# Graph sums by slots: four transfers per part and a new division of the 98 edge chunks

## The chip, the cores and the metric

The kernel runs on one core of a Trainium2 chip. The metric is the device time of one execution in microseconds (us). The engines are named as in the profile: PE (matmul) with PEld (its weight loads), DVE (VectorE), ACT (ScalarE), POOL (GpSimd) and SP (SyncE, which here only issues DMA transfers). The core has 16 DMA engines, which all queues share.

## The reference

A graph layer with 6250 nodes of 64 features and 200,000 edges of 64 features. The edges are sorted by `dst`; `src` is in no order.

```python
in_agg = segment_sum(edge_feat, receivers, num_segments=6250)   # receivers = dst
out_agg = segment_sum(edge_feat, senders, num_segments=6250)    # senders = src
to_updater = concatenate([in_agg, out_agg, node_feat], axis=1)  # 192 wide
h = relu(to_updater @ W1 + b1)                                  # 256 wide
x = layernorm(x + h @ W2 + b2)
```

Nearly all of the time goes into the two segment sums. The sum by `dst` is cheap, because a chunk of sorted edges touches a narrow window of nodes. The sum by `src` is the hard one: its rows have to reach nodes all over the table.

## The kernel before

The edges are cut into 98 chunks of 2048, laid out as 128 partitions by 16 columns. Every chunk is split into three bf16 parts that add up to the fp32 value (`split_hi`, `split_rest`, `split_mid`, `split_lo`), and its sum by `dst` is one set of 48 matmuls against a one-hot of the window (`sum_windows`, line 1632). For the sum by `src` there are two ways.

- *Scattered.* Within one column, edges with the same node are added up by a matmul with a 128x128 matrix of equal nodes (`same_nodes` on DVE, `payload_quad` on PE and ACT), and POOL then adds the 128 rows to a table in HBM by one indirect DMA (`add_chunk`, line 756). Four columns are a quad. There are four tables, and a scatter waits for the one before it on its table.
- *Shared.* Twelve of the sixteen columns of a chunk are sorted, six columns at a time, into slots: DVE builds a one-hot `to_slot` (line 1270), PE moves the edges (line 1656), ACT takes the result out of PSUM (line 851) and SP stores it in HBM as `slot_tiles`. Each of 22 groups of 286 nodes has 64 slots in such a tile, so a pair of groups fills 128 partitions. Later the tiles are loaded again, DVE or ACT builds a one-hot of 128 x 286 (`to_node`, lines 1309 and 917), and PE adds the tile to the sums of its pair of groups in PSUM with six matmuls (`sum_tiles`, line 1680).

The stages are: 4 early chunks that are scattered whole, while the slots of all edges are computed; 82 *sharing* chunks in a hardware loop, each with 4 columns scattered and 12 shared; 12 *summing* chunks (written out, not a loop), each scattered whole (the last with 12 of its columns), between whose steps the tiles of the 11 pairs of groups are summed; and a last stage of 13 steps with the two dense layers and the norm.

With 82 sharing chunks and two tiles from each there are 164 tiles per pair and 1804 in all. `SUM_FROM` says at which tile each summing chunk begins. A summing chunk has four steps, q = 0 to 3. In steps 0 to 2 it does one quad and 12 tiles (`LEAD`); in step 3 the last quad and the rest of its tiles, which run without other work between them. A pair's sums leave PSUM through ACT (`flush`, line 948) once its last tile is in, and are folded and put in place in the next chunk (`fold`, `put_sums`).

The tiles of a pair come in 8 parts of 20 or 21 tiles, into a ring of 4 buffers `slots_in`. SP issues the load of part k when PE has finished part k - 4 (`step`, `load_part`, `load_tiles`, lines 607 and 611), as three transfers: one into partitions 16 to 111, from the 8 slots that each of six columns has for each of the two groups, and two into partitions 0 to 15 and 112 to 127, from the slots that the columns share. DVE reads a part's node numbers (`relative`, line 1281) when it begins the tiles of the part before. It runs up to 24 tiles ahead of PE (`OH_BUFS`). The first four parts are loaded in halves beside the last eight pairs of sharing chunks.

## Time and profile before

| | us |
|---|---|
| median of 3 runs | 1498.37 |
| lowest, highest | 1495.05, 1502.81 |
| the profiled execution, its own time | 1498.98 |
| its span in the trace | 1497.2 |
| DVE busy | 1253.8 (84%) |
| PE busy | 1200.7 (80%) |
| ACT busy | 1016.1 (68%) |
| POOL busy | 1011.9 (68%) |

The 1.8 us between the profiled execution and its span lie outside the trace. Busy shares are means over stages that have different limits: no engine is busy for the whole span, and the rows further down split it by stage. In the views, `[2.49 <-issue]` behind an instruction is idle time of its engine before it, in which it waited for nothing that the profile shows, and `[4.00 <-DMA ...]` names what ended the idle time.

### The profile page before, as it was taken

What the parts mean: (1) busy time and instruction counts of PE and PEld (TensorE: products, weight loads), DVE (VectorE), ACT (ScalarE), POOL (GpSimd) and SP (SyncE); (2) the same over time, 40 slices, a digit from 0 to 9 for tenths busy, and PEclk for the clock granted to TensorE, in tenths of its full rate; (3) what the DMA queues carried; (4) which work ended last, traced back from release to release, by engine and by line L of the source; (5) the groups of instructions that cost most, each with busy time, mean ns of one, the idle gap of its engine ahead of it and who ended that gap; (6) DMA issues with size and microseconds to landing.
All of it is one profiled execution on the core that took longest, in us unless ns stands there. A gap on an engine that the chain in (4) does not pass through costs nothing.

```text
span 1497.2 us, 65347 instructions
## 1 busy us (share of the span) xinstructions
PE 1200.7 (80%) x23743; PEld 1022.0 (68%) x23743; DVE 1253.8 (84%) x3739; ACT 1016.1 (68%) x2315; POOL 1011.9 (68%) x615
## 2 busy tenths in 40 slices
PE   3667588888989889888888787777778787777797
PEld 2636477777878778778777676576677676666643
DVE  6665799999999999999999787777778886777776
ACT  6334599899999999999888655445556564555443
POOL 4878888888888888888888774463364445435423
PEclk9977799999999999999999989998999999999998
DMA  8332599999999999999999998987898979778731
GB/s 292 31 39 17 92 214 218 204 217 215 219 217 211 217 216 215 218 213 222 240 237 238 214 169 169 190 171 156 173 201 188 198 169 191 169 159 168 164 117 58
DMA packets 260280, 270.44 MB, mean 181 GB/s; under 512 B 97907, under 2 KB 221396, under 8 KB 259926
## 3 DMA queue, kind: packets, MB, share of 16 engines
q1 hardware_dynamic: 174504, 240.40, 59.0%
q0 software_dynamic: 85472, 27.20, 24.0%
q8 instruction: 115, 1.88, 0.6%
q10 hardware_dynamic: 144, 0.60, 0.1%
q14 instruction: 45, 0.37, 0.1%
HBM read 151.35 MB, written 116.75 MB: 179 GB/s over the span
## 4 chain that ended last, share of the span: by engine, by line
PE 29%; issue 24%; DMA 23%; POOL 15%; DVE 6%; ACT 1%; SPq 1%; POOLq 1%; DVEq 0%; ACTq 0%
PE psum L1680 20%; DMA out_tables<-payload,target 18%; POOL out_tables L756 14%; DMA slots_in<-slot_tiles 3%; DVE to_node L1309 2%; PE psum L1852 1%; PE psum L1843 1%; DVE same L1336 1%; PE psum L1632 1%; PE psum L1702 1%; PE psum L1639 1%; PE psum L1656 1%; PE psum L1864 1%; PE psum L1595 1%; PE psum L1720 1%
## 5 line engine op out<-in xcount | busy, mean ns | idle before, releaser
L756 POOL DMA_INDIRECT out_tables<-payload,target x580 | 978.5, 1687 | 410.0 <-DVE target L1317 199.5
L1656 PE MATMUL psum<-parts,to_slot 128*128 128x194 bf16 x5084 | 489.4, 248 | 29.7 <-ACT slots_out L851 25.0
L1680 PE MATMUL psum<-to_node,slots_in 64*64 64x286 bf16 x10824 | 392.3, 299 | 108.2 <-issue 98.7
L1656 PEld LDWEIGHTS psum<-parts,to_slot 128*128 128x128 bf16 x5084 | 422.6, 98 | 62.7 <-ACT slots_out L851 48.8
L1680 PEld LDWEIGHTS psum<-to_node,slots_in 64*64 64x64 bf16 x10824 | 346.6, 113 | 147.9 <-issue 110.0
L851 ACT ACTIVATE slots_out<-psum 128x388 bf16<-128x388 f32 x984 | 406.6, 474 | 54.0 <-PE psum L1656 39.6
L1270 DVE TENSOR_SCALAR to_slot<-iota_h,slot 128x640 bf16<-128x640 f16 (+1 forms) x984 | 344.7, 397 | 17.6 <-PE psum L1656 14.4
L1309 DVE TENSOR_SCALAR to_node<-iota_h,slot_rel 128x286 bf16<-128x286 f16 x902 | 252.8, 303 | 7.2 <-PE psum L1680 5.0
L917 ACT ACTIVATE to_node<-apart 128x286 bf16<-128x286 bf16 x300 | 126.2, 436 | 143.6 <-PE psum L1680 142.9
L1309 DVE TENSOR_SCALAR to_node<-iota_rows,slot_rel 128x286 bf16<-128x286 f16 x602 | 207.6, 345 | 0.0
L909 ACT ACTIVATE apart<-iota_h,slot_rel 128x286 bf16<-128x286 f16 x300 | 143.6, 522 | 24.4 <-DVE slot_rel L1281 24.3
L1230 DVE TENSOR_TENSOR rest<-feat,parts 128x1024 f32<-128x1024 f32 x98 | 118.7, 1212 | 21.3 <-ACT parts L830 20.9
L1718 PE MATMUL psum<-parts,same 128*128 128x65 bf16 x580 | 76.3, 202 | 66.5 <-DVE same L1336 61.1
L868 ACT ACTIVATE payload<-psum 128x256 f32<-128x256 f32 x145 | 54.3, 375 | 101.5 <-PE psum L1720 94.0
L1235 DVE TENSOR_TENSOR parts<-rest,parts 128x1024 bf16<-128x1024 f32 x98 | 118.8, 1212 | 2.6 <-ACT parts L840 2.6
L1718 PEld LDWEIGHTS psum<-parts,same 128*128 128x128 bf16 x580 | 57.3, 102 | 90.8 <-issue 81.4
L1336 DVE TENSOR_TENSOR same<-psum,cols_code 128x512 bf16<-128x512 f32 x145 | 99.9, 689 | 20.8 <-PE psum L1639 13.3
L830 ACT ACTIVATE parts<-feat 128x1024 bf16<-128x1024 f32 x98 | 105.3, 1074 | 17.8 <-DMA feat<-in_edge_attr 8.3
L840 ACT ACTIVATE parts<-rest 128x1024 bf16<-128x1024 f32 x98 | 104.1, 1062 | 4.3 <-DVE rest L1230 4.3
L1632 PE MATMUL psum<-onehot,parts 128*64 128x64 bf16 x4704 | 101.8, 199 | 3.7 <-issue 3.7
L1632 PEld LDWEIGHTS psum<-onehot,parts 128*64 128x64 bf16 x4704 | 88.4, 114 | 21.2 <-issue 18.8
L1281 DVE SCALAR_TENSOR_TENSOR slot_rel<-slots_in,cst 128x20 f32<-128x20 bf16 x88 | 21.6, 246 | 86.1 <-DMA slots_in<-slot_tiles 85.7
(137 smaller groups left out, 977.2 us busy)
## 6 DMA issues: line engine op xcount, KB each, us to landing
slot_tiles<-slots_out SPq DMA_DIRECT2D x164, 388.0 KB
feat<-in_edge_attr SPq DMA_DIRECT2D x195, 256.0 KB
slots_in<-slot_tiles SPq DMA_DIRECT2D x42, 763.9 KB
slots_in<-slot_tiles SPq DMA_DIRECT2D x42, 727.5 KB
slot_tiles<-slots_out SPq DMA_DIRECT2D x82, 291.0 KB
slots_in<-slot_tiles SPq DMA_DIRECT2D x84, 127.3 KB
slots_in<-slot_tiles SPq DMA_DIRECT2D x84, 121.2 KB
out_tables<-payload,target POOLq DMA_INDIRECT x580
```

The lines of the kernel that those rows point to most:

```text
L756: e.indirect_dma_start(out_tab, at, payload[b][:, t, :], None, element_offset=k * TABLE_ROWS * D, compute_op=ALU.add).then_inc(s_tab[k], 16)
L851: e.activation(slots_out[b][:, g:g + n, m, :], ps_share[r % BANKS][:, 0:n * SLOT_W].rearrange("p (g w) -> p g w", w=SLOT_W), ACT.Copy).the ...
L909: e.activation(apart[:, n % APARTS, :], iota_h[:, 0:HOT], ACT.Abs, bias=slot_rel[p % RING][:, k:k + 1], scale=-1.0).then_inc(s_apart, 1)
L917: e.activation(to_node[:, node_buf(g, i), :], apart[:, n % APARTS, :], ACT.Relu, bias=1.0, scale=-1.0).then_inc(s_to_node_act, 1)
L1230: e.tensor_tensor(rest[:, :, :], feat[b][:, :, :], parts[b][:, :, 1:1 + D], ALU.subtract).then_inc(s_rest, 1)
L1235: e.tensor_tensor(parts[b][:, :, 1 + 2 * D:1 + 3 * D], rest[:, :, :], parts[b][:, :, 1 + D:1 + 2 * D], ALU.subtract).then_inc(s_lo, 1)
L1270: last = e.tensor_scalar(to_slot[m][:, COLUMN_FROM[k]:COLUMN_FROM[k + 1]], iota_h[:, 0:COLUMN_SLOTS[k]], slot[:, bass.ds(s, 1), MINI * m + ...
L1309: e.tensor_scalar(hot, numbers, slot_rel[p % RING][:, k:k + 1], None, ALU.is_equal).then_inc(s_to_node, 1)
L1632: last = e.matmul(ps_win[b][h], parts[b][:, t, 1 + k * D:1 + (k + 1) * D], onehot[b][:, t // 2, :, t % 2], start=(j == 0 and k == 0), stop ...
L1656: last = e.matmul(ps_share[r % BANKS][:, o:o + SLOT_W], to_slot[m][:, COLUMN_FROM[k] + t * P:COLUMN_FROM[k] + (t + 1) * P], parts[b][:, SH ...
L1680: return e.matmul(ps_groups[g % 2][h][cols, 0:HOT], slots_in[p % RING][rows, j - PART_FROM[p], D * k:D * (k + 1)], to_node[rows, node_buf( ...
L1718: e.matmul(ps_pay[:, o:o + D + 1], w, parts[b][:, t, 0:1 + D], start=True, stop=False)
```

## The change

The change has three parts.

1. `SUMS` goes from 12 to 16. There are 78 sharing chunks in place of 82, 156 tiles per pair in place of 164, and 1716 in all. Four more chunks are scattered whole among the summing chunks.
2. The borders of the summing chunks no longer follow the pairs. Before, the chunks took 20, 144 and then ten times 164 tiles, so that each pair ended with a chunk. Now they take 20, then fourteen times 110, and 156; a pair ends somewhere inside a chunk.
3. A part is loaded by four transfers in place of three, each into every fourth partition: transfer j takes the slots of columns 2j and 2j + 1 of both groups into partitions j, j + 4, j + 8, ...; the last takes the shared slots of both groups. The bytes are the same. A slot carries its node's number, so its place within its group's half of the partitions doesn't matter.

```diff
--- before.py
+++ after.py
@@ -94,7 +94,7 @@
 TILE_COLUMNS = [[(k, tiles.index(t)) for k, tiles in enumerate(COLUMN_TILES) if t in tiles] for t in range(NODE_PAIRS)]
 HOT = GROUP_NODES
 HOT_ROW = 26
-SUMS = 12
+SUMS = 16
 SHARE_CHUNKS = N_CHUNKS - FIRST - SUMS
 SHARE_PAIRS = SHARE_CHUNKS // 2
 TILES = SHARE_CHUNKS * MINIS
@@ -102,19 +102,18 @@
 FIRST_TILES = 20
 LAST_TILES = TILES
 LEAD = 12
-GROUP_ENDS = [(g + 2, 0) for g in range(NODE_PAIRS - 1)]
 SUM_AT = {0: 0, 1: FIRST_TILES, SUMS - 1: ALL_TILES - LAST_TILES, SUMS: ALL_TILES}
-SUM_AT.update({u: TILES * (g + 1) - LEAD * q for g, (u, q) in enumerate(GROUP_ENDS)})
 SUM_FROM = []
 for u in range(SUMS + 1):
     lo, hi = max(a for a in SUM_AT if a <= u), min(a for a in SUM_AT if a >= u)
     SUM_FROM.append(SUM_AT[lo] + (SUM_AT[hi] - SUM_AT[lo]) * (u - lo) // max(1, hi - lo) // 2 * 2)
-assert len(GROUP_ENDS) == NODE_PAIRS - 1 and SUM_FROM == sorted(SUM_FROM)
+assert SUM_FROM == sorted(SUM_FROM)
 RING = 4
 PARTS = 2 * RING
 PART_FROM = [TILES * k // PARTS for k in range(PARTS + 1)]
 PIECES = 2
-LOADS = 3
+LOADS = MINI // 2 + 1
+assert 2 * SHARED == 4 * HOMES[0] == P // LOADS
 PART_TILES = max(b - a for a, b in zip(PART_FROM, PART_FROM[1:]))
 SLOT_W = 3 * D + 2
 OH_BUFS = 24
@@ -603,13 +602,13 @@
                 lo = PART_FROM[p]
                 into = slots_in[p % RING][:, a - lo:z - lo, :].rearrange("p t w -> p (t w)")
                 homes = slot_rows[0:HOME_AT[MINI], :].rearrange("(k r) w -> r k w", k=MINI)
-                both = 2 * HOMES[0]
-                e.dma_start(into[SHARED:P - SHARED, :], homes[both * g:both * (g + 1), :, a * SLOT_W:z * SLOT_W]
+                both, shared = 2 * HOMES[0], 2 * SHARED
+                for j in range(LOADS - 1):
+                    e.dma_start(into[j:P:LOADS, :], homes[both * g:both * (g + 1), 2 * j:2 * j + 2, a * SLOT_W:z * SLOT_W]
+                                ).then_inc(s_slot_in[p % RING], 16)
+                at = HOME_AT[MINI] + shared * g
+                e.dma_start(into[LOADS - 1:P:LOADS, :], slot_rows[at:at + shared, a * SLOT_W:z * SLOT_W]
                             ).then_inc(s_slot_in[p % RING], 16)
-                for h in range(2):
-                    at = HOME_AT[MINI] + SHARED * (2 * g + h)
-                    e.dma_start(into[(P - SHARED) * h:(P - SHARED) * h + SHARED, :], slot_rows[at:at + SHARED, a * SLOT_W:z * SLOT_W]
-                                ).then_inc(s_slot_in[p % RING], 16)
 
             def load_part(g, p):
```

The queue of SP at the start of the summing chunks, before: the loads of the parts (lines 607 and 611) behind those of the edges (line 595).

```order
L595 DMA feat<-in_edge_attr 128x512 x2
L607 DMA slots_in<-slot_tiles 96x1x3880
L611 DMA slots_in<-slot_tiles 16x3880 x2
L595 DMA feat<-in_edge_attr 128x512 x2
L607 DMA slots_in<-slot_tiles 96x1x4074
L611 DMA slots_in<-slot_tiles 16x4074 x2
```

And now:

```order
L594 DMA feat<-in_edge_attr 128x512 x2
L607 DMA slots_in<-slot_tiles 32x1x3686 x3
L610 DMA slots_in<-slot_tiles 32x3686
L594 DMA feat<-in_edge_attr 128x512 x2
L607 DMA slots_in<-slot_tiles 32x1x3880 x3
L610 DMA slots_in<-slot_tiles 32x3880
```

The places in the queue are the same; a part of 20 tiles has 3880 elements a row (21 tiles had 4074, 19 have 3686) and goes out as four transfers of 32 rows.

PE in the last step of a summing chunk, before: its last matmuls of equal nodes (line 1720), the second fold (line 1702), the window sums (line 1632), then all the tiles that are left (line 1680) and the next chunk's first quad.

```order
L1720 MATMUL psum<-parts,same 128x64 x2
L1639 MATMUL psum<-rows_code,ident_bf 128x512
L1702 MATMUL psum<-halves_sum,fold_mat 64x286
L1632 MATMUL psum<-onehot,parts 64x64 x48
L1680 MATMUL psum<-to_node,slots_in 64x286 x768
L1639 MATMUL psum<-rows_code,ident_bf 128x512
L1718 MATMUL psum<-parts,same 128x65
```

And now, in a chunk behind one in which a pair ended:

```order
L1719 MATMUL psum<-parts,same 128x64 x2
L1638 MATMUL psum<-rows_code,ident_bf 128x512
L1701 MATMUL psum<-halves_sum,fold_mat 64x286
L1631 MATMUL psum<-onehot,parts 64x64 x48
L1679 MATMUL psum<-to_node,slots_in 64x286 x444
L1638 MATMUL psum<-rows_code,ident_bf 128x512
L1717 MATMUL psum<-parts,same 128x65
```

The free run at the end of a chunk falls from 768 matmuls (128 tiles) to 444 (74 tiles); what stands around it is unchanged.

## Rows read from the trace of the kernel before

**Rows 1.** Windows by stage: us, then busy (x) by engine, PEclk, DMA share, GB/s
```profile
206.00:682.00 476.00, 422.99 (x7235) 377.09 (x7233) 466.84 (x1115) 434.27 (x997) 404.15 (x236) 1.00 0.98 215
...
842.30:1417.20 574.90, 448.95 (x12037) 386.80 (x12037) 445.20 (x1717) 310.03 (x756) 297.02 (x190) 0.93 0.85 177
1417.20:1497.20 80.00, 63.82 (x332) 31.39 (x331) 54.60 (x224) 29.45 (x56) 24.17 (x26) 0.93 0.29 89
```

**Rows 2.** Timeline of DVE: start, us; L1259 once a sharing chunk
```profile
308.89 0.68 DVE L1259 TENSOR_TENSOR onehot<-rel,iota_twice 128x1024 bf16<-128x1024 bf16 x1
...
316.98 0.68 DVE L1259 TENSOR_TENSOR onehot<-rel,iota_twice 128x1024 bf16<-128x1024 bf16 x1
```

**Rows 3.** Timeline of DVE: L1259 in summing chunks 0, 1 and 11
```profile
842.30 0.68 DVE L1259 TENSOR_TENSOR onehot<-rel,iota_twice 128x1024 bf16<-128x1024 bf16 x1
...
853.87 0.68 DVE L1259 TENSOR_TENSOR onehot<-rel,iota_twice 128x1024 bf16<-128x1024 bf16 x1
...
1368.61 0.68 DVE L1259 TENSOR_TENSOR onehot<-rel,iota_twice 128x1024 bf16<-128x1024 bf16 x1
```

**Rows 4.** Groups of DVE, 853.87 to 1368.61 (ten whole chunks): busy, mean ns, idle
```profile
L1309 DVE TENSOR_SCALAR to_node<-iota_h,slot_rel 128x286 bf16<-128x286 f16 x810 | 226.9, 303 | 6.9 <-PE psum L1680 4.7 <-issue 0.4
L1309 DVE TENSOR_SCALAR to_node<-iota_rows,slot_rel 128x286 bf16<-128x286 f16 x540 | 186.3, 345 | 0.0
L1336 DVE TENSOR_TENSOR same<-psum,cols_code 128x512 bf16<-128x512 f32 x41 | 28.1, 685 | 10.4 <-PE psum L1639 8.6 <-issue 1.4
L1230 DVE TENSOR_TENSOR rest<-feat,parts 128x1024 f32<-128x1024 f32 x10 | 12.2, 1224 | 19.5 <-ACT parts L830 19.2 <-issue 0.3
L1235 DVE TENSOR_TENSOR parts<-rest,parts 128x1024 bf16<-128x1024 f32 x10 | 12.2, 1219 | 0.0
L1281 DVE SCALAR_TENSOR_TENSOR slot_rel<-slots_in,cst 128x21 f32<-128x21 bf16 x39 | 9.9, 254 | 69.5 <-DMA slots_in<-slot_tiles 69.5
...
L1259 DVE TENSOR_TENSOR onehot<-rel,iota_twice 128x1024 bf16<-128x1024 bf16 x10 | 6.8, 680 | 0.0
```

**Rows 5.** Waits, 853.87 to 1417.2: us in total, times, longest
```profile
PE psum L1680 <- issue: 98.7, 48, 4.4
DVE slot_rel L1281 <- DMA slots_in<-slot_tiles: 85.7, 36, 5.2
...
DVE rest L1230 <- ACT parts L830: 19.2, 7, 5.5
```

**Rows 6.** Timeline of SP's queue and DVE: one part's load and its reader
```profile
978.49 0.57 SPq L607 DMA_DIRECT2D slots_in<-slot_tiles  x1
979.10 1.05 SPq L611 DMA_DIRECT2D slots_in<-slot_tiles  x2
...
986.39 0.26 DVE L1281 SCALAR_TENSOR_TENSOR slot_rel<-slots_in,cst 128x21 f32<-128x21 bf16 x1 [4.00 <-DMA slots_in<-slot_tiles]
```

**Rows 7.** Windows of half a microsecond over a load that runs alone
```profile
969.00:969.50 0.50, 0.46 (x16) 0.46 (x20) 0.00 (x0) 0.00 (x0) 0.00 (x0) 1.00 0.90 357
969.50:970.00 0.50, 0.50 (x13) 0.16 (x6) 0.00 (x0) 0.00 (x0) 0.00 (x0) 1.00 1.23 341
970.00:970.50 0.50, 0.50 (x14) 0.44 (x12) 0.30 (x1) 0.00 (x0) 0.00 (x0) 1.00 1.05 248
...
971.00:971.50 0.50, 0.50 (x6) 0.07 (x8) 0.50 (x4) 0.50 (x2) 0.00 (x0) 0.50 1.42 248
```

**Rows 8.** Page, part 6: the loads of a 20-tile part, KB each
```profile
slots_in<-slot_tiles SPq DMA_DIRECT2D x42, 727.5 KB
...
slots_in<-slot_tiles SPq DMA_DIRECT2D x84, 121.2 KB
```

**Rows 9.** Timeline of POOL: first and last of 16 scatters, next chunk's first
```profile
1287.10 1.60 POOL L756 DMA_INDIRECT out_tables<-payload,target  x1 [22.12 <-DVE target L1317]
...
1317.21 1.55 POOL L756 DMA_INDIRECT out_tables<-payload,target  x1 [0.31 <-DMA out_tables<-payload,target]
1340.39 1.55 POOL L756 DMA_INDIRECT out_tables<-payload,target  x1 [21.64 <-DVE target L1317]
```

**Rows 10.** DMA queues, 853.87 to 1417.2: packets, MB, share
```profile
q8 instruction: 96, 1.57, 1.3%
```

**Rows 11.** Timeline of POOL and DVE at the end of the sums
```profile
1404.56 1.57 POOL L756 DMA_INDIRECT out_tables<-payload,target  x1 [0.30 <-issue]
...
1426.48 0.86 DVE L1521 TENSOR_TENSOR aggT<-aggT,psum 64x256 f32<-64x256 f32 x2 [7.33 <-PE psum L1824]
```

## The prediction

> **What bounds the kernel now.** I read the page for the shares of busy time, then windows by stage, then the waits of the stage that looked loose, then single loads. The windows [rows 1] show two stages of different kinds. In the sharing loop DVE is busy 466.84 of 476.00 us: DVE is the bound there, and a chunk takes what its DVE work takes, 316.98 - 308.89 = 8.09 us from one to the next [rows 2]. In the summing stage, 842.30 to 1417.20, no engine is full: DVE 445.20 and PE 448.95 of 574.90 us, and the DMA engines are at 0.85. So there the time is work plus waits. On DVE, which builds the one-hots that PE consumes, the idle time is 574.9 - 445.2 = 129.7 us; 85.7 of it, in 36 waits of 2.38 on the mean, ends when a part of the slots lands [rows 5], and 44.0 has other reasons, 19.2 of it a wait of `rest` for ACT's `parts`. The reader should see from [rows 6] how the wait comes about: SP issues a part's transfers at 978.49, as soon as PE has set its buffer free, and DVE goes on at 986.39, 7.9 us later, of which it stood 4.0.
>
> PE has idle time of its own there: 98.7 us in 48 pieces, in which it waits for nothing that the profile shows [rows 5], while the queue that carries instructions moves 96 packets [rows 10]. 448.95 + 98.7 = 547.7 us is close to the 574.9 of the stage; this caps what a shorter wait on DVE can give.
>
> The sum is made against the profiled execution, 1498.98 us, 0.6 above the median of 1498.37; the 1.8 outside its span stay.
>
> **Part 1: four chunks leave the sharing loop.** The loop is DVE-bound and steady, so each chunk is worth its distance: 4 x 8.09 = -32.4 us [rows 2]. Their feature loads, stores of slots and 16 scatters go with them and give nothing more, since they lie beside DVE. The stage ahead of the loop works on 78 in place of 82 chunks per array; I cost that at nothing, with -2 to 0 as bounds.
>
> **Part 2: the summing stage gets four chunks and loses 88 tiles.** First the work on DVE, from its groups [rows 4]. One whole chunk costs 4 x 0.685 (`same`) + 1.22 (`rest`) + 1.22 (`parts`) + 0.68 (`onehot`) = 5.9 us. What is left of DVE's busy time belongs to the tiles: (445.2 - 12 x 5.9) / 1804 = 0.208 us each (one in six is built by ACT). So 4 x 5.9 - 88 x 0.208 = 23.6 - 18.3 = +5.3 us. On PE the same exchange is near zero: 528 matmuls on `slots_in` leave, and 4 chunks' equal-node and window matmuls come in.
>
> Second, the idle time of DVE that has other reasons: 44.0 us over 12 chunks is 3.7 a chunk, so four more bring +14.7. Against this stands the new border. Before, each pair ended with its chunk, so that ACT's `flush`, which waits for PE's last tile of the pair, stood in its queue just ahead of the `split_hi` for which `rest` then waits (19.2 us, 7 times [rows 5]). Now most flushes fall inside the free run of tiles and `split_hi` isn't behind them. I take half of the 19.2 as gone, -9.6, with 0 and -19.2 as bounds. What is late instead is ACT's own sixth tile behind the flush; up to 12 tiles of cover stand before it. Sum of both: +5.1 us.
>
> Third, the waits for parts. They arise where DVE runs faster than parts come, that is in the free run at a chunk's end; 36 in 12 chunks is 3 a chunk. The run falls from 128 tiles to 74, and I take 2.5 waits a chunk in the 15 chunks that have one: 38. With a load as before they would sum to 38 x 2.38 = 90.4 us, +4.7.
>
> **Part 3: the four transfers.** The trace shows no such load, so it is bounded. A part of 20 tiles is 727.5 + 2 x 121.2 KB [rows 8], 993 thousand bytes. A load that runs alone [rows 7] starts at 357 and 341 GB/s and then falls to 248 for the rest, with DMA shares near or above 1: the engines are occupied by transfers that don't get on. That isn't the limit of the source, which had just given 357. The later packets include the two transfers into 16 neighbouring partitions. If all of it ran at 357, it would take 2.8 us in place of the 4.0 at 248: -1.2 us is the upper bound of the gain. The lower bound is a loss: a fourth issue of about 0.5 us (two issues took 1.05 [rows 6]) that nothing repays, +0.5. I take -0.8, nearer to the row at 341, since the ramp at the start stays and a neighbour's load is often in flight. A wait of 2.38 becomes 1.58, 38 of them 60.0: 60.0 - 85.7 = -25.7 us for the parts' waits in all.
>
> What the rows suggest by their rates, the Trainium skill explains: by "SBUF — State Buffer", section "Door 1: The DMA port swizzle", a partition's number picks one of 16 ports, partitions 0 to 15 reach four of them and 112 to 127 four others, while every fourth partition reaches all sixteen. By its 27.2 GB/s a port, eight ports would give 218 (an estimate from that page); the trace's 248 is higher, but the trace agrees that a load with few ports is slower. The same page's "Summary: rules for kernel authors" speaks against the change: one DMA and not several, as each pays a fixed cost. By it the load would be no faster; that is the last rival's case. The trace disagrees at least in part: the 7.9 us of [rows 6] hold all three issues, which follow one another within 1.6 us.
>
> **The sum.** Summing stage: +5.3 + 5.1 - 25.7 = -15.3, so 559.6 us. Its 14 middle chunks then take (559.6 - 11.6 - 46.5) / 14 = 35.8 us each: 11.6 is the first chunk (853.87 - 842.30) and 46.5 the last, now 48.6 for 164 tiles (1417.20 - 1368.61 [rows 3]) less eight tiles. In all -32.4 - 15.3 = -47.7: 1498.98 - 47.7 = **1451 us**. At the end, POOL's last scatter is issued at 1404.56 and the first use of the tables is at 1426.48, in which DVE waits 7.33 for PE [rows 11]; the last chunk's scatters may start some 8 us later behind the chunk before, and this cover takes it.
>
> **Rivals.**
> - *The scatters set the pace.* A chunk's 16 scatters take 1317.21 - 1287.10 + 1.86 = 32.0 us, and now POOL waits some 22 us for the next ones [rows 9], in chunks of 51.5. At 35.8 a chunk POOL is nearly full. For it: an indirect write queues behind part loads, and there are more beside each other now. Against it: 32.0 is below 35.8. If a scatter takes 0.3 more, 36.8 a chunk, the stage takes 11.6 + 14 x 36.8 + 46.5 = 573 us: 1498.98 - 32.4 - 1.6 = 1465.
> - *The load is no faster* (PE's rate or the source is its limit). The waits are 90.4: +4.7 + 5.3 + 5.1 = +15.1, 1482. For it: 248 is also what the sharing loop's mix reaches at most, 215 on the mean [rows 1].
> - *Freer DMA engines also shorten PE's unexplained stands*, and waits fall to 0.9 each: 34 - 85.7 = -51.5, a stage of 534 and 1425. PE's 448.95 of work and half of its stands make 498, so PE would allow it. Against it: a chunk would be down to 34.0 us, two above the 32.0 that its scatters take (first rival).
> - *Slower: the start of a load decides.* A chunk's first wait is the longest (4.0 in [rows 6]), because DVE is 24 tiles ahead as the free run begins, and there are now 16 such starts. With the fourth issue added and 3 waits in each of 15 chunks, 45 x 2.9 = 130 us (+45); with the four chunks' other idle time in full (+14.7) and DVE's work, the stage takes +65 and the kernel 1499 - 32.4 + 65 = 1532. It decides from +32.4 on, that is from about 98 us of waits for parts.
>
> **How the numbers follow.** Forecast 42% (its own range 1438 to 1464), scatters 13%, no faster load 20%, freer engines 15%, slower 10%. The range that should hold 8 in 10 takes the scatters' case, most of the case without a faster load and half of the fourth: 1428 to 1488. A change under 0.5% (7.5 us) can't be told from none. Faster by more: 42 + 13 + 15 + 13 of the 20 = 83%. Within: the other 7 and 2 of the last case, 9%. Slower: 8%.
>
> **What would show it.** In the sharing loop L1259 stays 8.09 us apart and the summing stage begins near 810. Middle summing chunks lie near 36 us apart. A load that runs alone holds above 300 GB/s to its end, and DVE's reader starts about 7 us after the issue in place of 7.9. Waits for `slots_in` are near 60 us, and `rest` waits for ACT under 12. The prediction is wrong if POOL has no waits left for `target` (then the scatters bound), if loads still fall to 248, or if a middle chunk's idle time on DVE is much over the 7 us that I count (3.7 + 2.5 x 1.58 = 7.7, less 0.6 for the flush).

## The result, and the profile after

The changed kernel takes 1384.12 us, median of 4 runs (1378.47 to 1385.26), against 1497.89 of the kernel before in the same set: a ratio of 0.9212 with a 95% interval of 0.9169 to 0.9254. The forecast was 1451 with a range of 1428 to 1488. The direction was right and the gain more than twice as large as forecast: 114 us instead of 48. The profiled execution took 1384.06 us with a span of 1382.3, and all sums below are made in it.

The windows of the changed kernel by stage (us, then busy time by engine: PE, PEld, DVE, ACT, POOL, then PEclk, DMA share, GB/s) answer to [rows 1]:

```profile
206.00:682.00 476.00, 423.03 (x7198) 377.28 (x7197) 469.32 (x1119) 434.88 (x1001) 404.08 (x237) 1.00 0.98 217
803.48:1304.00 500.52, 422.39 (x11909) 357.45 (x11909) 450.20 (x1682) 313.19 (x770) 405.60 (x254) 0.98 0.86 204
1304.00:1382.30 78.30, 63.67 (x331) 31.37 (x331) 54.84 (x224) 28.74 (x54) 24.17 (x26) 0.92 0.29 90
```

The sharing loop looks as before. The summing stage is 500.52 us long instead of 574.90, although it has four chunks more. DVE works 450.20 us in it (445.20 before), so what went is idle time. PEclk rose from 0.93 to 0.98, both close to the higher of the clock's two levels; PE's busy time fell from 448.95 to 422.39. POOL went from 297 to 406 us and from 52% to 81% of the stage.

The timeline of DVE, L1258 once a chunk (L1259 before), answers to [rows 2, 3]:

```profile
306.19 0.68 DVE L1258 TENSOR_TENSOR onehot<-rel,iota_twice 128x1024 bf16<-128x1024 bf16 x1
314.28 0.68 DVE L1258 TENSOR_TENSOR onehot<-rel,iota_twice 128x1024 bf16<-128x1024 bf16 x1
...
803.48 0.68 DVE L1258 TENSOR_TENSOR onehot<-rel,iota_twice 128x1024 bf16<-128x1024 bf16 x1
815.22 0.68 DVE L1258 TENSOR_TENSOR onehot<-rel,iota_twice 128x1024 bf16<-128x1024 bf16 x1
...
1257.26 0.68 DVE L1258 TENSOR_TENSOR onehot<-rel,iota_twice 128x1024 bf16<-128x1024 bf16 x1
```

A sharing chunk is again 8.09 us from the next. The summing stage begins at 803.48, which is 38.8 us earlier. Its 14 middle chunks take (1257.26 - 815.22) / 14 = 31.6 us each; 35.8 was forecast.

Waits in the summing stage, 803.48 to 1304 (us in total, times, longest), and below them the other waits of DVE in it, answer to [rows 5]:

```profile
PE psum L1679 <- issue: 57.6, 59, 2.2
DVE slot_rel L1280 <- DMA slots_in<-slot_tiles: 35.1, 19, 4.7
...
POOL out_tables L755 <- DVE target L1316: 11.4, 5, 3.2
POOL out_tables L755 <- DMA out_tables<-payload,target: 5.7, 12, 1.3
```

```profile
DVE same L1335 <- PE psum L1638: 4.3, 8, 0.9
DVE to_node L1308 <- PE psum L1679: 1.5, 4, 0.8
DVE rest L1229 <- ACT parts L829: 0.7, 1, 0.7
```

The waits for parts fell from 36 to 19 and from 2.38 to 1.85 us on the mean. `rest` waited 19.2 us for ACT and now 0.7. PE's stands without a releaser fell from 98.7 to 57.6 us, and the longest from 4.4 to 2.2.

The groups of DVE in the 14 middle chunks (busy, mean ns, idle before) answer to [rows 4]:

```profile
L1308 DVE TENSOR_SCALAR to_node<-iota_h,slot_rel 128x286 bf16<-128x286 f16 x770 | 221.6, 310 | 1.5 <-PE psum L1679 1.5
...
L1335 DVE TENSOR_TENSOR same<-psum,cols_code 128x512 bf16<-128x512 f32 x57 | 38.8, 681 | 2.6 <-PE psum L1638 2.0
L1280 DVE SCALAR_TENSOR_TENSOR slot_rel<-slots_in,cst 128x20 f32<-128x20 bf16 x78 | 18.3, 235 | 31.5 <-DMA slots_in<-slot_tiles 31.2 <-issue 0.3
```

Before, in ten chunks, `to_node` stood 6.9 us and `same` 10.4; now 1.5 and 2.6 in fourteen. One part's load in the timeline of SP's queue, and its reader on DVE, answer to [rows 6]; the issues of the fourth transfer (L610) stand behind the three of L607:

```profile
864.86 2.30 SPq L607 DMA_DIRECT2D slots_in<-slot_tiles  x3
867.20 0.60 SPq L610 DMA_DIRECT2D slots_in<-slot_tiles  x1
...
871.19 0.25 DVE L1280 SCALAR_TENSOR_TENSOR slot_rel<-slots_in,cst 128x19 f32<-128x19 bf16 x1 [2.62 <-DMA slots_in<-slot_tiles]
```

From the first issue to the reader it is 6.33 us, 7.90 before, though SP now needs 2.94 us to issue the load. The two rows overstate the gain, since this part has 19 tiles and that of [rows 6] had 21. Over all 84 whole parts, from the first issue to the end of the last packet (worked out from the records of single packets), the median load took 7.25 us before and takes 6.29 now, and between 880 and 1230 us the median packet of 7760 bytes took 0.49 us before and takes 0.31 now. Windows of half a microsecond over this load answer to [rows 7]:

```profile
868.50:869.00 0.50, 0.50 (x25) 0.50 (x20) 0.06 (x1) 0.37 (x1) 0.34 (x1) 1.00 1.24 327
869.00:869.50 0.50, 0.50 (x25) 0.50 (x19) 0.00 (x0) 0.00 (x0) 0.35 (x1) 1.00 1.15 349
869.50:870.00 0.50, 0.50 (x26) 0.50 (x19) 0.00 (x0) 0.47 (x2) 0.50 (x1) 1.00 0.97 265
870.00:870.50 0.50, 0.50 (x27) 0.50 (x20) 0.00 (x0) 0.50 (x2) 0.50 (x1) 1.00 0.91 188
```

The rate still falls below 248 before the reader starts; at that time the next part's load begins too, so this row can't tell the two apart. The timeline of POOL in the stage answers to [rows 9]:

```profile
1129.65 1.55 POOL L755 DMA_INDIRECT out_tables<-payload,target  x1 [0.31 <-issue]
1131.51 1.55 POOL L755 DMA_INDIRECT out_tables<-payload,target  x1 [0.30 <-issue]
...
1146.36 2.62 POOL L755 DMA_INDIRECT out_tables<-payload,target  x1 [0.30 <-DMA out_tables<-payload,target]
1149.29 1.55 POOL L755 DMA_INDIRECT out_tables<-payload,target  x1 [0.30 <-issue]
```

The scatters now follow one another at 1.86 us across the chunk borders. 16 x 1.86 = 29.8 us is the least that a chunk can take, and one takes 31.6. At the end of the sums (timelines of POOL and DVE) [rows 11] have changed too:

```profile
1297.03 1.55 POOL L755 DMA_INDIRECT out_tables<-payload,target  x1 [0.30 <-issue]
...
1304.89 0.69 DVE L1501 TENSOR_TENSOR feat<-feat 128x512 f32<-128x512 f32 x1 [6.86 <-DMA feat<-out_tables]
```

The last scatter is issued 7.9 us before the first use of the tables, and DVE waits 6.86 us for their load. Before, DVE's first use of the tables was not the L1521 of [rows 11] but L1502 at 1416.94, 12.4 us after the last scatter, and no wait for a DMA stood ahead of it. So the cover was 12.4 us and not 22, it is used up, and the wait for the tables now closes the summing stage: 6.0 of its 500.52 us, 1298.03 to 1304.00, are this wait. The last stage is not longer (78.3 us, 80.0 before).

### The profile page after: what moved, and what is told of

It is laid out like the page before. It is cut to its first block, busy times and chain, and to the rows that moved or that the text cites. A ratio compares the mean times of both kernels' runs of the same rounds, so it can differ in the third digit from the quotient of the medians.

```text
span 1382.3 us, 63667 instructions
## 1 busy us (share of the span) xinstructions
PE 1144.7 (83%) x23123; PEld 967.7 (70%) x23123; DVE 1225.5 (89%) x3629; ACT 988.0 (71%) x2259; POOL 1093.0 (79%) x663
## 4 chain that ended last, share of the span: by engine, by line
PE 30%; DMA 24%; issue 20%; POOL 13%; DVE 9%; SPq 1%; ACT 1%; POOLq 1%; DVEq 0%; ACTq 0%
DMA out_tables<-payload,target 21%; PE psum L1679 18%; POOL out_tables L755 12%; DVE to_node L1308 4%; DMA slots_in<-slot_tiles 2%; PE psum L1655 1%; PE psum L1851 1%; PE psum L1631 1%; PE psum L1638 1%; DVE same L1335 1%; PE psum L1719 1%; PE psum L1842 1%; DMA feat<-in_edge_attr 1%; PE psum L1701 1%; PE psum L1863 1%
## 5 line engine op out<-in xcount | busy, mean ns | idle before, releaser
L755 POOL DMA_INDIRECT out_tables<-payload,target x628 | 1059.6, 1687 | 220.7 <-issue 163.9
L1655 PE MATMUL psum<-parts,to_slot 128*128 128x194 bf16 x4836 | 466.0, 248 | 21.1 <-ACT slots_out L850 14.4
L1655 PEld LDWEIGHTS psum<-parts,to_slot 128*128 128x128 bf16 x4836 | 403.1, 98 | 51.8 <-ACT slots_out L850 38.6
L850 ACT ACTIVATE slots_out<-psum 128x388 bf16<-128x388 f32 x936 | 386.6, 474 | 50.1 <-PE psum L1655 37.5
L1679 PE MATMUL psum<-to_node,slots_in 64*64 64x286 bf16 x10296 | 354.3, 286 | 66.8 <-issue 57.6
L1679 PEld LDWEIGHTS psum<-to_node,slots_in 64*64 64x64 bf16 x10296 | 306.1, 107 | 103.2 <-issue 73.3
L1269 DVE TENSOR_SCALAR to_slot<-iota_h,slot 128x640 bf16<-128x640 f16 x936 | 328.9, 398 | 13.9 <-PE psum L1655 9.4
L1308 DVE TENSOR_SCALAR to_node<-iota_rows,slot_rel 128x286 bf16<-128x286 f16 x572 | 191.3, 334 | 0.0
L916 ACT ACTIVATE to_node<-apart 128x286 bf16<-128x286 bf16 x286 | 118.0, 436 | 72.8 <-PE psum L1679 70.2
L1631 PEld LDWEIGHTS psum<-onehot,parts 128*64 128x64 bf16 x4704 | 89.1, 115 | 19.2 <-issue 16.7
L1719 PE MATMUL psum<-parts,same 128*128 128x64 bf16 x1256 | 86.0, 199 | 0.6 <-issue 0.6
```

Source lines behind the costliest of these rows:

```text
L755: e.indirect_dma_start(out_tab, at, payload[b][:, t, :], None, element_offset=k * TABLE_ROWS * D, compute_op=ALU.add).then_inc(s_tab[k], 16)
L850: e.activation(slots_out[b][:, g:g + n, m, :], ps_share[r % BANKS][:, 0:n * SLOT_W].rearrange("p (g w) -> p g w", w=SLOT_W), ACT.Copy).the ...
L1269: last = e.tensor_scalar(to_slot[m][:, COLUMN_FROM[k]:COLUMN_FROM[k + 1]], iota_h[:, 0:COLUMN_SLOTS[k]], slot[:, bass.ds(s, 1), MINI * m + ...
L1308: e.tensor_scalar(hot, numbers, slot_rel[p % RING][:, k:k + 1], None, ALU.is_equal).then_inc(s_to_node, 1)
L1631: last = e.matmul(ps_win[b][h], parts[b][:, t, 1 + k * D:1 + (k + 1) * D], onehot[b][:, t // 2, :, t % 2], start=(j == 0 and k == 0), stop ...
L1655: last = e.matmul(ps_share[r % BANKS][:, o:o + SLOT_W], to_slot[m][:, COLUMN_FROM[k] + t * P:COLUMN_FROM[k] + (t + 1) * P], parts[b][:, SH ...
```

## The experiments

The chips of the experiments ran the kernel before in 1537 to 1574 us and not 1498, so everything is compared by ratios to it. There the sharing loop isn't bound by DVE all the time: between 206 and 682 us a chunk takes 8.2 to 9.1 us on the mean, by kernel, which is looked at below. A ratio mixes this with what an edit does to the summing stage. So the stage's own length is given too: from the one-hot (L1258) of its first chunk to DVE's first use of the tables, 574.6 us before and 501.4 after in the first measurement.

**The change in its parts.** The four transfers alone, in the kernel before:

```
-LOADS = 3
+LOADS = MINI // 2 + 1     (and the loads of the changed kernel)
```

> The kernel before with the four transfers alone (12 summing chunks, borders at the pairs). Theory L, by which the loads are most of what the forecast missed: a part's load takes more than 0.8 us off each wait, DVE's waits for slots_in fall from 85.7 us to under 45, PE's idle time on issue from 98.7 to under 75, and the kernel takes 1430 to 1450 us. Rival B, by which the shorter free runs and the new borders are what did it: the waits stay above 60 us and the kernel takes 1465 to 1480.

Ratio 0.9739 (0.9686 to 0.9791). Both signs of theory L came (waits for parts 34.9 us, PE's stands 62.1), but the time, some 1459 us by the ratio, lies between its 1450 and rival B's 1465. The sixteen chunks with even borders, and three transfers as before:

```
-SUMS = 12
+SUMS = 16                 (GROUP_ENDS and its SUM_AT.update(...) left out)
```

> The changed kernel with the three transfers of before (16 summing chunks, even borders). Theory L: what is left is the exchange of chunks, 1440 to 1465 us, with waits for slots_in of 70 us and more. Rival B: under 1415 us, since 16 chunks and even borders keep most of the gain.

Ratio 0.9636 (0.9582 to 0.9690), some 1443 us and so inside theory L's time; its waits for parts are 55.9 us and not 70, and rival B is refuted. Only the even borders (GROUP_ENDS left out), with 12 chunks and three transfers:

> 12 summing chunks as before, with even borders (20, ten or so times 162, 164 tiles) and three transfers. If the flush ahead of split_hi cost what I took (half of 19.2 us): 1488. If the border is worth nothing: 1494 to 1502. Rival B: under 1475.

Ratio 1.0012 (0.9966 to 1.0057): the border is worth nothing. Even borders and the four transfers, with 12 chunks:

> 12 summing chunks with even borders and four transfers. Both theories: the time of the kernel with four transfers alone, less what the borders gave by themselves. The distance from here to the changed kernel's 1384 is the price of moving four chunks: forecast -32.4 us for the sharing loop and +10 for work and other idle time, about -20 in all; if the scatters set the pace in the new one, less.

Ratio 0.9764 (0.9688 to 0.9840), the same as the four transfers alone. The changed kernel itself, on a chip of this kind, with nothing edited:

> The changed kernel again, to have it on the chip of the runs beside it. 0.921 of the kernel before as on the first chip. If the parts simply add (0.974 for the loads alone, 0.964 for chunks and borders with three transfers), 0.938: anything below that is a gain that only both together give.

Ratio 0.9438 (0.9348 to 0.9527), and 0.9356 and 0.9364 in two later sets. The 0.921 expected for it did not come in any of them: part of the first measurement's gain is missing on these chips, and why is open. (In that measurement PE is busy 354.3 us with the tile matmuls of the summing stage, here 392.0 with the same ones.) The product of the parts, 0.9739 x 0.9636 = 0.9385, lies within the interval, but the ratios can't say that the parts are independent. The profiles split them (us; the last column is the stage less DVE's work and less the waits for parts):

| chunks, borders, transfers | stage begins | stage length | waits for parts | DVE's other idle time |
|---|---|---|---|---|
| 12, at the pairs, four | 912.3 | 547.4 | 34.9 | 62.5 |
| 12, even, three | 903.4 | 580.8 | 69.4 | 60.2 |
| 12, even, four | 897.8 | 548.6 | 35.9 | 63.6 |
| 16, even, three | 850.9 | 575.3 | 55.9 | 64.8 |
| 16, even, four (changed kernel, another chip) | 849.8 | 530.9 | 34.8 | 41.9 |

With three transfers, the move of four chunks shortens the run by 61.0 us (spans 1569.8 and 1508.8), but 52.4 of them arise before the stage begins, in a loop that takes some 9 us a chunk here, and 5.5 in the stage. The four transfers alone take 32.2 us off the stage. DVE's other idle time stays at 60 to 65 us with either part by itself and is 41.9 only with both (40.0 in the last set). That is an effect which neither part has alone, as far as runs on different chips can show it.

Waits over the whole run show what each part does. First the four transfers in the kernel before (33 waits for parts, 21 of `rest`):

```profile
DVE slot_rel L1282 <- DMA slots_in<-slot_tiles: 34.9, 33, 2.0
DVE rest L1231 <- ACT parts L831: 21.1, 21, 2.5
```

Then sixteen chunks with three transfers, and only the even borders:

```profile
DVE slot_rel L1279 <- DMA slots_in<-slot_tiles: 55.9, 34, 3.9
...
DVE rest L1228 <- ACT parts L828: 3.7, 8, 1.0
```

```profile
DVE slot_rel L1279 <- DMA slots_in<-slot_tiles: 69.4, 41, 3.8
DVE rest L1228 <- ACT parts L828: 10.2, 11, 2.3
```

The transfers halve the waits for parts (69.4 to 35.9 us with 12 chunks and even borders in both), from 41 to 29 waits and from 1.7 to 1.2 us each. Sixteen chunks lower them too, with three transfers (55.9 us, 34 waits). The even borders take the wait of `rest` from 21.1 to 12.3 us (four transfers in both), near the prediction's half; sixteen chunks take it on to 3.9 (from 10.2 to 3.7 with three transfers), and the prediction had no term for that. The wait of `same` for PE goes another way: sixteen chunks raise it, from 19.4 to 30.7 us with three transfers, and the four transfers lower it, to 6.7 with 12 chunks and 8.8 with 16. The wait of `to_node` for PE is 23.7 and 22.2 us with three transfers (12 and 16 chunks), 30.8 and 15.4 with four.

**Where the transfer's bytes go.** Four transfers as before, each into 32 neighbouring partitions. The rows of a part land in other partitions than the sums want:

```
-e.dma_start(into[j:P:LOADS, :], homes[...]
+e.dma_start(into[P // LOADS * j:P // LOADS * (j + 1), :], homes[...]
```

> The changed kernel with its four transfers of 32 rows into 32 neighbouring partitions each in place of every fourth; half of the slots then stand in the wrong group's half, so the sums by src are not those of the reference, and the work is the same. Theory P, by which it is where the rows land: the load is as slow as with three transfers or slower, waits for slots_in double to 60 us and more, time 2.5% to 5% above the changed kernel. Rival N, by which the number or size of the transfers is what helped: within 0.5% of the changed kernel.

0.9522 (0.9433 to 0.9611), 0.9% above the changed kernel of its set, with 56.2 us of waits for parts and not 34.8. The intervals overlap, and the stage is 532.3 us long against 530.9. So the packets and the waits move nearly as theory P says (0.51 us against 0.31), but not the time, for which it wanted 2.5% and more; rival N isn't excluded by it. One transfer of 128 neighbouring rows of the table (again other rows than the sums want):

```
+e.dma_start(into, slot_rows[P * g:P * g + P, a * SLOT_W:z * SLOT_W])
```

> The changed kernel with a single transfer of 128 rows per part, 128 neighbouring rows of the slot table into the 128 partitions; these are not the rows of the part's groups, so the sums by src are not those of the reference, the bytes and the work are the same. By the rule of one transfer and not several: the fastest of the three forms, 0.5% to 1.5% below the changed kernel. By theory P: all 128 partitions are reached by one transfer, so it is within 1% of the changed kernel. Rival N: slower, as it has the fewest.

0.9144 (0.9063 to 0.9226), 3.1% below the changed kernel of its set (0.9144 / 0.9438), with 10.5 us of waits for parts in 12 waits and 30.4 us of stands of PE. Here the rule of one transfer was right, beyond its 0.5% to 1.5%. So either one transfer is better than four, or neighbouring rows are better than rows in blocks. To tell, I numbered the shared slots so that a part is one regular block pattern and a single transfer can fetch the right rows:

```
-e.scalar_tensor_tensor(shared[:, k, :], group[:, k, :], float(SHARED - h), taken_i[:, k, :], ...
+later = (rank + taken > SHARED - 0.5) * (HOME_AT[1] - HOMES[0])
+e.tensor_tensor(shared[:, k, :], later, taken_i[:, k, :], ALU.add)
+rows = slot_rows.rearrange("(k r) w -> r k w", k=8)
+e.dma_start(into, rows[both * g:both * (g + 1), :, a * SLOT_W:z * SLOT_W])
```

> Changed kernel, but the second half of each group's shared slots is numbered 176 rows further on, so that the shared slots look like two more columns of homes; a part then comes by ONE transfer of 128 rows, from blocks at a 176-row stride, into neighbouring partitions. Two small DVE instructions more per batch of ranks (about 1 us in all). Theory A (the number of transfers is what cost): as the one-transfer kernel of the second set, 3% below the changed kernel (0.97), slot_rel's waits for the DMA near 10 us instead of 35, PE's stands on issue near 30 instead of 55 us, packets near 0.35 us. Theory B (it was the 128 neighbouring rows of the table that made that kernel fast): nothing gained, within 1% of the changed kernel, packets at 0.39 us or more. Theory C (neighbouring partitions slow a transfer down, whatever their number): slower than the changed kernel by 1%, slot_rel waits 50 us and more.

It took 0.9681 (0.9629 to 0.9734) against 0.9356 (0.9311 to 0.9400) of the changed kernel, whose expectation was

> The changed kernel again, as the yardstick of this set. Ratio to the kernel before 0.92 (as the first measurement) to 0.944 (as in the second set); summing chunks of 31 to 34 us.

That is 3.5% slower where theory A wanted 3% faster. A is refuted, and B expected no loss; only C has the right sign, but it expected 1%. The last set takes the same numbering of slots, and so the same bytes, by four, two and one transfer (`into[j:P:LOADS, :]` with LOADS = 4, 2, 1), beside the changed kernel.

> The changed kernel once more, as the yardstick of this set: ratio 0.92 to 0.944 to the kernel before, median packet of a part near 0.30 us.

> The shared slots numbered as in the one-transfer kernel (so all 128 rows of a part are in blocks at a 176-row stride), but a part comes by four transfers into every fourth partition, as in the changed kernel. Theory A (the order in which an engine's packets go over the partitions decides): as the changed kernel within 1%, median packet 0.30 us, waits of slot_rel near 35 us. Theory B (the stride of the table's rows is slow, the 32 neighbouring shared rows had helped): 2 to 3% slower than the changed kernel, median packet 0.5 us.

> The same bytes by two transfers into every second partition. Theory A: between the two ends, 1 to 3% slower than the changed kernel, median packet 0.35 to 0.5 us, since an engine then writes neighbouring pairs of partitions two times in a row. Theory C (only one single transfer is slow, by a form of its own): as the changed kernel or up to 1% faster, median packet 0.30 us.

> The same bytes by one transfer, run again beside the others: 3% slower than the changed kernel (0.968 of the kernel before in the last set), median packet 0.54 us, waits of slot_rel near 50 us, if the first measurement holds.

| kernel | ratio to before | stage, us | waits for parts, us | stands of PE, us | median load, us | median packet of 7760 bytes, us |
|---|---|---|---|---|---|---|
| changed kernel | 0.9364 (0.9274 to 0.9453) | 527.7 | 33.9 | 46.5 | 6.17 | 0.32 |
| four, every fourth partition | 0.9402 (0.9315 to 0.9489) | 527.5 | 30.5 | 50.5 | 6.19 | 0.31 |
| two, every second partition | 0.9594 (0.9502 to 0.9687) | 544.8 | 37.1 | 64.4 | 6.15 | 0.47 |
| one, all partitions in order | 0.9678 (0.9595 to 0.9760) | 575.3 | 53.0 | 83.7 | 6.39 | 0.56 |
| *second set:* changed kernel | 0.9438 (0.9348 to 0.9527) | 530.9 | 34.8 | 55.3 | 6.25 | 0.31 |
| four, neighbouring partitions | 0.9522 (0.9433 to 0.9611) | 532.3 | 56.2 | 55.8 | 6.83 | 0.51 |
| one, neighbouring rows | 0.9144 (0.9063 to 0.9226) | 497.9 | 10.5 | 30.4 | 4.47 | 0.29 |

(The packets' medians are taken from the records of single packets between 880 and 1230 us, those of the loads, from first issue to end of the last packet, from all 84 whole parts.) The row of SP's queue among the DMA queues in these 350 us (packets, MB, share of 16 engines), first with four transfers and then with one, sums the packets up:

```profile
q1 hardware_dynamic: 14066, 61.67, 58.7%
```

```profile
q1 hardware_dynamic: 10254, 56.27, 68.5%
```

61.67 / 0.587 = 105 and 56.27 / 0.685 = 82: for the same share of the engines' time, four transfers move 28% more. The windows of the same stretch, again four and then one:

```profile
880.00:1230.00 350.00, 306.70 (x7916) 238.96 (x7913) 301.07 (x1112) 210.00 (x515) 265.26 (x168) 1.00 0.83 195
```

```profile
880.00:1230.00 350.00, 282.16 (x7250) 226.84 (x7252) 274.62 (x1014) 191.64 (x470) 242.06 (x154) 0.94 0.89 178
```

The forecasts of theory A came in this set (the median packet and the time of all three), and B is refuted: four transfers from the same rows are as fast as the changed kernel. For a packet's length the order and place of the partitions is shown to matter, with number, size and source of the transfers the same: 0.31 us into every fourth partition, 0.51 into neighbouring ones. For the kernel's time it is not shown.

From four to two to one, the number of transfers and the order of the partitions change together. The kernel with four transfers into neighbouring partitions has packets nearly as long as the one-transfer kernel (0.51 and 0.56 us), and its stage is 43 us shorter (532.3 and 575.3) and no longer than with every fourth partition. That speaks for the number of transfers, though the two kernels number the slots differently; four transfers with the new numbering into neighbouring partitions were not run. The load as a whole doesn't explain the stage either: with one transfer it takes 0.2 us more than with four, and the stage 48 us more. PE's granted clock is 0.94 in the stretch above with one and 1.00, the higher of its two levels, with four, and whether that is a cause or follows from its stands is open too.

The Trainium skill ("SBUF — State Buffer", section "Door 1: The DMA port swizzle") counts only how many ports a transfer's partitions reach, which is all sixteen for 128 partitions in one transfer and for every second or fourth one. By it the kernels with four, two and one transfers of the new numbering are equal; the measurement decides against that. The same page's "Summary: rules for kernel authors" wants one transfer and not several; here one is 2.9% slower than four (0.9678 / 0.9402). In the kernel of 128 neighbouring rows one transfer was the fastest of all, as the rule wants it. I did not show why the two differ; this stays open.

**Scatters and the count of chunks.** The scatters of the last four columns in every summing chunk but the last are left out (60 of 628; what they would write is missing):

```
-for t in range(mode.cols):
+for t in range(COLS - QUAD if mode.sums else mode.cols):
```

> The changed kernel without the scatters of the last four columns of the summing chunks (60 of 628 left out, so those rows are missing from the sums by src); all else is done. Theory S, by which POOL's 16 scatters at 1.86 us set the pace of 31.3 us a chunk: a chunk falls to 29 to 30 us, DVE's work of 28.8 us being next, and the kernel gains 15 to 30 us. Rival D, by which DVE's own work and waits set it: under 6 us.

0.9312 (0.9197 to 0.9428), 1.3% below the changed kernel of its set; the intervals overlap. In the profiles the stage is 15.5 us shorter (515.4 and 530.9), the low end of theory S, but a middle chunk only falls from 33.7 to 32.5 us and not to 30; POOL then waits 157.2 us for `target` and not 58.3. On these chips the scatters' pace costs about this much. In the first measurement, with chunks of 31.6 us, POOL has less to spare, and no run tests it there. Eighteen chunks, in the kernel with one transfer:

> The one-transfer kernel with 18 summing chunks instead of 16. Theory A (the DVE's work per chunk sets the pace, the sharing loop's 8.09 us a chunk is saved): 2 x 8.09 less 2 x 5.9 of DVE work = 4 us faster than with 16, 0.3%. Theory B (GpSimd's scatters set the pace of the summing chunks once the loads are cheap, 16 scatters of 1.9 us in each of them): the summing stage grows by 2 x 30 us less what the tiles gave, 1 to 2% slower than with 16, and GpSimd waits for its targets under 10 us in the stage.

0.9759 (0.9710 to 0.9807), 0.8% slower than sixteen in the same kernel (0.9681). The stage grew by 24.2 us (565.7 to 589.9), and POOL doesn't wait for `target` in it any more (53.3 us with sixteen): theory B's direction and sign, a little under its size in time. The ratio is blurred by the loop, in which a chunk took 8.89 us here and 8.46 with sixteen. Fourteen chunks (SUMS = 14) in the changed kernel:

> The changed kernel with 14 summing chunks instead of 16 and everything else kept. Theory A (DVE's work and the parts): 2 x 8.09 more in the sharing loop, 2 x 5.9 less DVE work and some more waiting for parts, 0.3 to 1% slower than the changed kernel. Theory B (the scatters of whole chunks already hold it back): 60 us of scatters fewer in the stage for 16 us more of sharing, the same or up to 1% faster than the changed kernel; GpSimd's waits for its targets rise from 30 to over 100 us.

0.9709 (0.9669 to 0.9749), 3.8% slower than sixteen, outside both theories. Its profile puts the surplus not into the summing stage but into the sharing loop: POOL's group of scatters between 250 and 750 us, first in the changed kernel of the first measurement, then in the changed kernel of the last set, then with fourteen chunks:

```profile
L755 POOL DMA_INDIRECT out_tables<-payload,target x248 | 427.2, 1723 | 75.6 <-issue 58.8 <-DMA out_tables<-payload,target 16.8
```

```profile
L755 POOL DMA_INDIRECT out_tables<-payload,target x235 | 429.5, 1828 | 72.7 <-issue 59.8 <-DMA out_tables<-payload,target 12.9
```

```profile
L755 POOL DMA_INDIRECT out_tables<-payload,target x221 | 423.2, 1915 | 79.2 <-issue 63.4 <-DVE target L1316 13.1 <-DMA out_tables<-payload,target 2.7
```

In all three, busy time and gaps nearly fill the 500 us; with fourteen chunks 13.1 us of the gaps are waits for DVE. With four scatters a chunk that is 500 / 248 x 4 = 8.06 us, where DVE is as full, then 500 / 235 x 4 = 8.51 and 500 / 221 x 4 = 9.05, where POOL sets most of the pace. (The changed kernel on the chip of the fourteen chunks is like that of the last set: 234 scatters of 1821 ns.) Over 80 sharing chunks the last 0.54 us are some 43 us, most of the difference. Why the same scatters take 1821 ns in one build and 1915 in the other is not settled, so the time doesn't say what two chunks are worth. The stages do, as an estimate: 521.5 us with fourteen and 527.7 to 530.9 with sixteen, and 17 us for two sharing chunks of 8.5, make fourteen slower by 8 to 11 us, or 0.5% to 0.7%, inside theory A.

The only kernels below the changed one take other rows than the sums want or leave scatters out; four transfers with the new numbering equal it, and none of the whole computation beat it.

## Why the prediction was wrong

**Sharing loop.** -32.4 forecast. The chunks are 8.09 apart as read, but the stage begins 38.8 us earlier. 2.7 of the other 6.4 are there at 306.19 already (308.89 before), 2.2 of them at the first sharing chunk: the stage ahead of the loop, costed at nothing with -2 as its bound, gave that. The rest arises in the loop's last chunks. Small, and of the same sign as everything else.

**DVE's work in the summing stage.** 445.2 + 5.3 = 450.5 forecast, 450.20 measured. The exchange of 4 chunks against 88 tiles was sized to 0.3 us.

**DVE's idle time for other reasons: a failed step.** It kept 3.7 us a chunk for sixteen chunks, less half of the wait of `rest`: 44.0 + 5.1 = 49.1 us. Measured are 500.52 - 450.20 - 35.1 = 15.2, so 33.9 us less; and 6.0 of the 15.2 are the wait for the tables at the end, which the prediction put at nothing (its cover of 22 us was 12.4). `rest` waits 0.7 us (19.2 before), `same` 4.3 (12.1) and `to_node` 1.5 (5.0). What failed is that the chunks and the transfers were priced each by itself. With three transfers, the runs with 12 and 16 chunks have 60.2 and 64.8 us of this idle time, +4.6 where the prediction has +5.1; with four transfers it is 63.6 and 41.9, the last on another chip. For `rest` the count of chunks does it; `same` is freed by the transfers and not by the shorter runs of tiles. Why the sum falls only with both is open, and so is why it falls lower in the first measurement than on the other chips.

**Waits for parts: the other failed step.** 38 waits of 1.58 us, 60.0 in all, were forecast; 19 of 1.85 came, 35.1 in all, 24.9 us less. The length was near enough. The count was wrong: I multiplied waits per chunk by chunks and let a faster load shorten each wait only. The parts' runs show what both do to the count: sixteen chunks take it from 41 to 34 with three transfers (55.9 us in place of 69.4, where the prediction has +4.7), and the four transfers take it from 41 to 29 with 12 chunks, and each wait from 1.7 to 1.2 us. The transfers' share, 69.4 - 35.9 = 33.5 us, is close to the 30.4 forecast. Nor did the waits fall evenly before: in ten chunks the 39 parts of 21 tiles [rows 4] had 69.5 us of them and the 40 parts of 20 tiles 8.7; now the parts of 20 and 19 tiles have 14.8 and 16.4. So they hung on where in a chunk a part fell, and an average per chunk hides that. That a load which lands about 1 us earlier makes short waits vanish whole fits this; it was not tested by itself.

**The sum of the misses.** 6.4 + 33.9 + 24.9 + 1.7 (the last stage) = 66.9 us, and 1451 - 67 = 1384. Half of it is the first failed step, over a third the second. None of the misses cancels another.

**The rivals.** That freer DMA engines also shorten PE's stands had 15% and came true: 98.7 to 57.6 us, in a stage shorter than its 534. Its argument against, that a chunk can't go near the 32.0 us of its scatters, was taken from the wrong row: that sum held a gap, and scatters that never wait come 1.86 us apart, 29.8 a chunk. The scatters' rival has its place (POOL is near its limit: 11.4 us of waits for `target`, 178.3 before) but not its price; there are still such waits, so its sign did not come fully. That the load is no faster is refuted by the four transfers alone (69.4 to 35.9 us of waits), and that the start of a load decides by 35.1 us where it needed 98. The sign "a lone load holds above 300 GB/s" wasn't seen: the rate falls to 188, beside the next load, so this row neither shows nor refutes the prediction's reason, few partitions in the last transfers. The price of the transfers came out near the forecast (33.5 us for 30.4) without that reason being shown.

## What to carry to other kernels

Don't carry an idle time per chunk or a count of waits over to a schedule with other run lengths and other loads at once: ask for each wait how late its releaser is, and what is left if that margin grows by what the change gives; a wait shorter than that may go whole. When a change has two parts, ask which waits need both. How a load is cut into transfers and in which order it serves the partitions changed packets, waits and time here with the same bytes, but not in step with one another; measure two or three forms before settling on one transfer, and look at the length of the stage and not only at the packets. Compare stages as well as whole times, since another stage can run at another pace in the next build. When the bound of a loop is read, add gaps to busy time on the engine that only issues: 427 us of scatters and 76 of gaps in 500 is as full as DVE.

## What the runs showed of the hardware

- The same 128 rows by four, two or one transfer (into every fourth, every second and all partitions) took 0.31, 0.47 and 0.56 us a packet of 7760 bytes, the summing stage 527.5, 544.8 and 575.3 us, and the kernel 0.940, 0.959 and 0.968 of the time before. The whole load took 6.19, 6.15 and 6.39 us.
- Four transfers of 32 rows into neighbouring partitions had packets of 0.51 us, into every fourth partition 0.31, and the stage was 532.3 and 530.9 us.
- PE's stands without a releaser moved with the loads' form (83.7, 64.4 and 50.5 us for one, two and four). The instruction queue moved 97 packets in the whole summing stage both before and after, while the stands fell from 98.7 to 57.6 us. Long packets alone don't do it: with four transfers into blocks of partitions they were 0.51 us and the stands 55.8 us.
- The time of a scatter in the sharing loop differs from measurement to measurement and from build to build on one chip (1723 ns in the changed kernel's first profile, 1821 and 1915 above), and where it is well above 1723 ns, at which POOL and DVE are equally full, POOL sets most of the loop's pace.
- The issues of one part took SP 1.66 us with three transfers [rows 6] and 2.94 with four, and the part was there no later for it.
